# Attention rows split in their own layout and transposed by DMA, softmax taken earlier in VectorE's step, block maxima at five spread places

## The reference

```python
x = hidden                                   # (1, 2048, 1024)
# attention part: layernorm, q k v, and attention over the 32 HEADS of one token
n = layernorm(x)
q, k, v = (n @ w.T + b  reshaped to (S, 32, 32) for each of wq, wk, wv)
scores = einsum('bshd,bstd->bsht', q, k) / sqrt(32)
x = x + einsum('bsht,bstd->bshd', softmax(scores), v)
# feed-forward part: weights quantised to NF4 by blocks of 64 (absmax) and back
n = layernorm(x)
h = silu(n @ dq(w1).T) * (n @ dq(w2).T)      # 2752 wide
out = x + h @ dq(w3).T
```

## Time and profile before

| | us |
|---|---|
| median of 3 runs | 2148.68 |
| profiled execution, its own time | 2147.14 |
| span of the profiled execution | 2145.3 |
| busy: PE / DVE / ACT / POOL | 1989.0 / 1841.1 / 1492.3 / 1167.7 |
| first projection matmul | 87.29 |
| first feed-forward matmul | 721.15 |

### The profile page before, as it was taken

How to read it: one execution, slowest core, us unless ns; L and a number is a source line. 1 busy time by engine, 2 the same in 40 slices (tenths; PEclk the granted TensorE clock), 3 DMA queues, 4 the chain that set the end, 5 groups by cost and what they waited for, 6 DMA issues and landing times. The chain is left out here.

```text
span 2145.3 us, 30875 instructions
## 1 busy us (share of the span) xinstructions
PE 1989.0 (93%) x10272; PEld 1074.2 (50%) x10272; DVE 1841.1 (86%) x1846; ACT 1492.3 (70%) x1665; POOL 1167.7 (54%) x674
## 2 busy tenths in 40 slices
PE   5699999999987599999999999999999999999998
PEld 3477777776767244444444444444444444444442
DVE  8578888888878999898989989899998989989882
ACT  5424242424226697988989889797988979989782
POOL 0100101010111578788787787878787787787873
PEclk8799999999986699999999999999999999999999
DMA  7123433343322741212121212121212121212113
GB/s 284 58 77 113 142 113 128 116 137 113 122 74 98 267 126 40 59 39 52 45 53 45 59 39 59 39 59 39 59 39 59 39 53 45 59 40 55 35 35 157
DMA packets 219616, 175.24 MB, mean 82 GB/s; under 512 B 143664, under 2 KB 186672, under 8 KB 219568
## 3 DMA queue, kind: packets, MB, share of 16 engines
q1 hardware_dynamic: 217456, 166.23, 27.5%
q10 hardware_dynamic: 2112, 8.39, 1.0%
HBM read 115.34 MB, written 25.17 MB: 65 GB/s over the span
## 5 line engine op out<-in xcount | busy, mean ns | idle before, releaser
L1272 DVE SCALAR_TENSOR_TENSOR bank<-signs,bank 128x1024 f32<-128x1024 int8 (+2 forms) x792 | 964.4, 1218 | 102.2 <-ACT signs L1171 75.2
L1171 ACT ACTIVATE signs<-w_nat,compare_bias 128x1024 int8<-128x1024 f32 (+2 forms) x924 | 987.4, 1132 | 0.8 <-DVE w_nat L1272 0.6
L1402 PE MATMUL bank<-x2T_hi,w12T_hi 128*128 128x512 f16 x1376 | 524.2, 381 | 17.2 <-DVE hidden L1280 6.6
L1403 PE MATMUL bank<-x2T_lo,w12T_hi 128*128 128x512 f16 x1376 | 524.0, 381 | 0.0
L1404 PE MATMUL bank<-x2T_hi,w12T_lo 128*128 128x512 f16 x1376 | 523.8, 381 | 0.0
L772 PE MATMUL bank<-wT_hi,xT_hi 128*128 128x512 f16 x768 | 298.0, 388 | 12.2 <-issue 12.2
L772 PE MATMUL bank<-wT_hi,xT_lo 128*128 128x512 f16 x768 | 297.8, 388 | 0.0
L1423 PE MATMUL bank<-w3T_hi,hT_hi 128*128 128x512 f16 x704 | 272.3, 387 | 25.6 <-DVE hidden L1280 22.5
L727 ACT ACTIVATE probs<-probs 128x1024 f32<-128x1024 f32 x16 | 16.9, 1058 | 375.1 <-DVE probs L653 375.1
L1425 PE MATMUL bank<-w3T_hi,hT_lo 128*128 128x512 f16 x704 | 272.3, 387 | 0.0
L1424 PE MATMUL bank<-w3T_lo,hT_hi 128*128 128x512 f16 x704 | 271.7, 386 | 0.0
(11 more groups left out here) (96 smaller groups left out, 2670.9 us busy)
## 6 DMA issues: line engine op xcount, KB each, us to landing
ff_raw<-in_L_ffn_w SPq DMA_DIRECT2D x63, 512.0 KB, 3.7
w_nat<-in_L_ffn_w SPq DMA_DIRECT2D x63, 512.0 KB, 3.9
x_nat<-in_L_attn_hidden_states SPq DMA_DIRECT2D x16, 512.0 KB, 3.8
x_res<-in_L_attn_hidden_states SPq DMA_DIRECT2D x16, 512.0 KB, 4.4
x<-x_res SPq DMA_DIRECT2D x16, 512.0 KB, 2.6
acc<-x ACTq DMA_DIRECT2D x4, 2048.0 KB, 15.1
out<-acc SPq DMA_DIRECT2D x16, 512.0 KB, 2.6
w_raw<-in_L_attn_wq SPq DMA_DIRECT2D x8, 512.0 KB, 6.9
```

Of the source, the lines that this page charges most:

```text
L1171: nc.scalar.activation(signs[0:rows, ring(v, k), 0:cols], w_nat[0:rows, v % SLOTS, 0:cols], ACT.Sign, scale=COMPARE[SUMMED[k]][0], bias=co ...
L1272: V.scalar_tensor_tensor(to, part, HALF_STEP[SUMMED[k]], total, ALU.mult, ALU.add).then_inc(sign_used, 1)
L1402: nc.tensor.matmul(dst, hi, x2T_hi[:, toks, c], start=c == 0, stop=False)
L1403: nc.tensor.matmul(dst, hi, x2T_lo[:, toks, c], start=False, stop=False)
```

## The change

1. **Split as the rows lie, transposed by DMA.** The normalised tile is no longer transposed by TensorE. ScalarE writes its high half and GpSimd its low half, 128x1024 each, into x_half (`high_half`, `low_half`), and ScalarE starts two DMA transposes into xT_hi and xT_lo (`turn_x`). TensorE waits for them by `x_ready`. The layernorm's scale takes in X_SCALE (`moments`). For the finished tile the same two halves go to DRAM untransposed, and `load_tokens` transposes the four blocks of 512 tokens by DMA on their way back; x2T_hi and x2T_lo are laid out by block.
2. **VectorE's order.** Row maxima and subtraction come after the first evacuation of Q, ahead of `norm_apply`; the block transpose of the exponentials comes right after the second one; the second layernorm's apply comes after the transpose of Q. The two `split_lo` are gone. qkv has two slots instead of three: V takes that of Q, so the first evacuation of each waits for the other's block transpose.
3. **TensorE's order.** Context has banks 6 and 7, so that the scores wait for `ctx_read` no more. The 32 scores stand at 8 places of Q, after its 7th to 14th matmul, four at each. p_diag is written in two parts (eight instructions of 32x512) and the first 16 context products wait only for the first.
4. **Looks at named places**: early, centered, summed, key, value. Nine in steps 0 and 1 together, five and four in a loop turn, three in step T - 2.

The diff, cut to its core:

```diff
+        x_half = sb("x_half", [P, 2, E], F16)
...
+        def high_half(act, rows, half, done):
+            nc.scalar.activation(half[:, 0], rows, ACT.Copy).then_inc(done, 1)
+
+        def low_half(pool, rows, half, done):
+            nc.gpsimd.tensor_tensor(half[:, 1], rows, half[:, 0], ALU.subtract).then_inc(done, 1)
+
+        def turn_x(act, n, slot):
+            for i, (to, done) in enumerate(((xT_hi, x_hi_done), (xT_lo, x_lo_done))):
+                act.wait_ge(done, n + 1)
+                act.sem_inc(held, 1)
+                act.dma_start_transpose(to[:, slot], x_half[:, i]).then_inc(x_ready, 16)
...
-        mixing = bank[:, 4:6].rearrange("p b n -> p (b n)")
-        scores = mixing.rearrange("p (t h) -> p t h", h=HEADS)
-        context = mixing.rearrange("p (t d) -> p t d", d=HD)
+        scores = bank[:, 4:6].rearrange("p b n -> p (b n)").rearrange("p (t h) -> p t h", h=HEADS)
+        context = bank[:, 6:8].rearrange("p b n -> p (b n)").rearrange("p (t d) -> p t d", d=HD)
...
+        LOOK_PLACES = {5: "early centered summed key value", 4: "early centered summed value", 3: "early centered summed", 0: ""}
...
@@ sync, step @@
-                for look in todo[1:4]:
-                    load_ff(*look)
+                for place in ("centered", "summed", "key"):
+                    load_for(place)
                 if end and attend:
-                    sp.wait_ge(x2_turned, 2 * (n - 1))
+                    sp.wait_ge(x2_lo_done, n - 1)
                     load_res(sp, n - 1)
-                for look in todo[4:]:
-                    load_ff(*look)
                 if end:
-                    sp.wait_ge(x2_lo_done, 2 * n)
+                    sp.wait_ge(x2_lo_done, n - 1)
                     sp.sem_inc(held, 1)
-                    for dram, part in ((x2_hi_dram, x2_hi), (x2_lo_dram, x2_lo)):
...
+                        sp.dma_start(dram[bass.ds((n - 2) * P, P), :], x2_half[:, i]).then_inc(x2_out, 16)
+                load_for("value")
@@ gpsimd, step @@
+                if normalize:
+                    pool.wait_ge(x_hi_done, n + 2)
+                    low_half(pool, x_nat[:, 1 - u], x_half, x_lo_done)
...
                 if feed and attend:
                     next(feed)
+                if end:
+                    pool.wait_ge(x2_hi_done, n - 1)
+                    low_half(pool, x_res[:], x2_half, x2_lo_done)
@@ scalar, step @@
                 if normalize:
-                    split_hi(act, n + 1, xT_hi[:, 1 - u], x_turned, x_hi_done)
+                    act.wait_ge(normed, n + 2)
+                    act.wait_ge(x_ready, 32 * (n + 1))
+                    high_half(act, x_nat[:, 1 - u], x_half, x_hi_done)
...
-                    place(p_diag, flipped[:], p_placed)
+                    place(p_diag, flipped[:], p_placed, 2)
+                if normalize:
...
+                    turn_x(act, n + 1, 1 - u)
...
-                    split_hi(act, n - 2, x2_hi, x2_turned, x2_hi_done)
+                    act.wait_ge(normed2, n - 1)
+                    high_half(act, x_res[:], x2_half, x2_hi_done)
@@ tensor @@
+                    if early:
+                        skip, slots = 6, skip
...
-                        if end:
-                            pe.wait_ge(ctx_read, n - 1)
...
-                        pe.wait_ge(p_placed, n)
+                        pe.wait_ge(p_placed, 2 * n - 1)
                         pe.wait_ge(v_ready, n)
+                        if end:
+                            pe.wait_ge(ctx_read, n - 1)
                     for t in range(first, last):
+                        if t == QUAD // 2:
+                            pe.wait_ge(p_placed, 2 * n)
...
-                    turn(x_nat[:, 1 - u], x_turned)
...
-                    turn(x_res[:], x2_turned)
@@ feed_forward, sync @@
             def load_tokens(b):
-                tiles = slice(b * ST_BLOCK, (b + 1) * ST_BLOCK)
+                if b == 0:
+                    sp.wait_ge(g["x_ready"], 32 * T)
                 for part, dram in ((x2T_hi, x2_hi_dram), (x2T_lo, x2_lo_dram)):
-                    sp.dma_start(part[:, tiles].rearrange("p t c s -> p t (c s)"),
...
+                    sp.dma_start_transpose(part[:, b], dram[b * BANK:(b + 1) * BANK, :]).then_inc(x2_in[b], 16)
```

## The result

The changed kernel takes 2183.36 us (median of 4 runs, 2182.59 to 2185.4), the kernel before in the same session 2147.95 (2145.85 to 2148.92). The ratio is 1.0168 [1.015, 1.0185]: slower by 1.7%, where about 1% faster was forecast, and the time lies outside the range. Each profiled execution can be cut at the marks that the prediction used: VectorE's first reading of a context, the one of tile 14 (M), and the first sum of weight tile 3.

The account below looks back on a forecast made before the run. TensorE was taken to bound the attention steps before, the chain to VectorE's value look (33.5 us a step) after. 2147.14 - 44.0 (attention) + 20.8 (hand-over) = 2123.9 us profiled, so 2125 as median; range 2102 to 2158.

Parts of the forecast that it names:

- TensorE's step: Attention step: TensorE needs 32.2 us, 3.8 less than before, if nothing else is late.
- The chain to the value look: Attention loop: VectorE's last look waits for apply, halves, stores and load; period 33.5 us, TensorE waiting some 1.3.
- Rival E: Attention loop: TensorE's wait grows past what the clock bears, 8 to 10 us lost a step, over 2220 us; 4%.
- Steps 14 and 15: Last attention steps: idle stretch of 3.69 us and low clock go; 65.9 us instead of 81.0, 15.1 saved.
- The start: Before the first context: TensorE begins 2 us later, step 1 gives back its transpose; 0.7 us lost.
- The hand-over: From M to the first sum of weight tile 3: 109.7 us against 88.9, so 20.8 given back.
- two forms for this stretch: Hand-over: 87.3 + 4 tau; from tau about 7, last block and second weight transpose bind, near 76 + 6 tau.
- tau: Hand-over: time of each 1 MB token block's transposing load, taken as 5.6 us, ends 2.6 and twice 5.6.
- ScalarE's cover: Attention step: issuing two DMA transposes, 2.5 us, hides under p_diag's 4.7 us and costs nothing.
- rival D: Attention loop: the two transposes are not hidden on ScalarE; period 36.3 us, + 34, 2159 us in all; 13%.
- rival C: Hand-over: token blocks move at the rate of plain copies, 2.6 us each; 12 us less, 2113; 17%.

Follow-up runs that it names:

- e1: Kernel after, with SyncE issuing the value look's load ahead of the residual's load and the two stores: 2130.12 us, 0.9926 of before.
- e9: Kernel after, with the value look's load ahead of the two stores only, still behind the low-half wait and the residual's load: 2158.2 us.
- e6: On e1, VectorE makes the looks at the feed-forward scales behind the exponentials' transpose and the row sums in step T - 1: 2126.03 us.
- e3: Kernel after, with the first tile's low half made by VectorE instead of GpSimd: 2187.88 us, 1.0197 of before.
- e2: Kernel after, with token blocks read by plain copies instead of transposing ones (output differs, for timing only): 2179.72 us.
- e7: Kernel after with value load first, first low half on VectorE, x1 store ahead of token blocks 1 to 3, and scales later, together: 2125.47 us.
- e8: On e7, SyncE issues the four acc loads behind all token blocks, and a later weight tile's load ahead of blocks 2 and 3: 2110.96 us.
- e4: Kernel after, with TensorE doing the first 8 products of V's first half once more each attention step: 2165.52 us.

## Why the prediction was wrong

**TensorE's step: right.** 32.2 us were worked out (with 96 x 0.22 = 21.1, where the text has 20.7, it is 32.6), 32.37 measured, where nothing is late (e1).

**The chain to the value look: the right chain, sized 1.5 us short.** The prediction named it link by link from one context read to the next and came to 33.5. In the step shown above the apply ends at + 23.1 (22.6 forecast), the low half at + 26.6 (25.9), the value load is issued at + 28.5 (27.3), lands at + 33.9 (32.3) and the period is 35.0. No link is off by more than 0.5. But the wait on TensorE is what is left over, the period less TensorE's step: 33.5 - 32.2 = 1.3 was forecast and 34.96 - 32.37 = 2.6 came. 12 x (34.96 - 33.5) = 17.5 of the 41.2 us that the loop missed.

**The clock: the step that failed.** The prediction put falls of the clock in the loop at nothing. Rival E had them with 4%, "this needs two other misses", and with a fall in each step. The row with a wait of 1.84 and the mean clock of 0.98 made 1.3 look safe. What came was a fall in three of twelve steps, 7.9 us each: 23.7. e9 shows that the miss of the chain was not needed for it: its loop steps without a fall take 33.72 us, close to the forecast 33.5, which leaves 33.72 - 32.37 = 1.35 for TensorE's wait, and its profiled run has two falls all the same, at waits of 2.25 and 1.82 us. The prediction reasoned with the mean wait, and single waits are longer. The trace of before had a sign of this that the prediction did not use. Right behind the two longest of these waits in its loop, 2.13 us at 380.29 and 2.09 at 452.35, the clock is at 0.50 for some 3 us, and the 0.98 of the earlier trace rows is one of these two:

```profile
381.60:384.80 3.20, 3.20 (x9) 1.25 (x8) 3.20 (x4) 3.14 (x5) 0.00 (x0) 0.50 0.00 0
```

The chain's delay and the falls are cured by the same edit (e1), so the chain and not the new packing of scores, the halves of p_diag or the transposes on ScalarE is what made the loop slower.

**Steps 14 and 15: 9.9 us short** (75.8 against 65.9). Step T - 1 takes 44.23 us from context read to context read where 32.4, TensorE's step, was put; what is left for step 14 is 31.6, no more than the 33.5 forecast. The idle stretch ahead of the scores is gone as forecast. A new one of 2.91 us stands ahead of the context products, since VectorE's looks at the scales stand ahead of the exponentials' transpose, and the low clock of the earlier trace rows comes back some 20 us later, counted from M. This accounts for the smaller part: e6, without that wait, saves 3.9 us in this step (44.71 in e1, 40.80 in e6). The other 8.4 above a plain step are there in e6 too, where VectorE is what is late and makes the feed-forward pieces. That these pieces are the cause is read from that window; no run takes them out. The prediction saw such pieces and their order for step T, and for T - 1 it put them at nothing.

**The start: 4.4 short.** The low half was priced, what GpSimd does between it and the all-reduce was not (e3).

**The hand-over: 4.3 short, otherwise right.** The store of x1 goes out at M + 72.4 (72.9 forecast), the last apply starts at + 75.8 (75.5), ScalarE's high half at + 88.2 (88.0). A token block alone takes 4.4 us and not 5.6, but the first had 1.5 MB ahead of it and took 6.7. What was missed is behind that: ScalarE stands 7.61 us where it issues the loads of acc, before it was 2.93. The prediction's two forms for this stretch meet at a tau of 5.65 and not at about 7 (87.3 + 4 tau = 76 + 6 tau); at the 5.0 us that the four blocks take in the mean here the first holds, so nothing hung on that.

**ScalarE's cover (rival D): held.** The two transposes of a tile are issued beside p_diag, and the finished tile's high half starts when p_diag ends (396.89 in the step shown above):

```profile
395.29 1.47 ACTq L272 DMA_TRANSPOSE xT_lo<-x_half  x1
...
396.94 1.06 ACT L263 ACTIVATE x_half<-x_res 128x1024 f16<-128x1024 f32 x1
```

**The transposes' rate (rival C): nearer the forecast than plain copies.** The Trainium skill ("Advanced Engine Details and Errata", X-Bar Transpose (TRN2)) has transposes as fast as plain copies. Here a block of 1.05 MB out of DRAM takes 4.4 us, some 238 GB/s, and copying the blocks in e2 was worth 11 us; the rows bear out that they are slower than plain copies, less so than the 187 GB/s that the prediction took from SBUF.

What stays open: what decides whether a wait is followed by a fall (below).

## What to carry to other kernels

A load that an engine on the critical path will wait for goes into a queue ahead of everything that waits for a late producer: the queue takes over the latest wait in it. Where TensorE is left with a pause of some 2 us each step, count a fall of the clock as likely and not as a tail risk; here the falls cost 23.7 us in the loop, beside 30.6 of the late chain. A mean wait is not enough for that: look at the longest single ones, and at the clock right behind them, already in the trace of before. Large transfers with slack (acc here) are to be spread, since small urgent ones stand behind them: in e7 those of another queue, in e8 those of the same one.

## What the runs showed of the hardware

- The length of the wait alone does not say whether the clock falls. In the kernel after waits of 2.34, 2.71, 4.61 and 2.91 us were followed by 0.50, one of 2.31 was not, nor were 2.09 and 1.89. In e9 waits of 1.82 and 2.25 were, in e3 one of 2.32 was and one of 2.42 was not. In the kernel before, 2.13 and 2.09 were followed by some 3 us at 0.50 only, while the falls in the loops of after, e3, e4 and e9 last 17 to 24 us.
- GpSimd's all-reduce ran at once after 12.34 us of waiting (e3), and 5.94 us after the end of a subtraction (after). The root behind a memset came after 6.96 us (6.89 in the kernel before).
- A transpose's issue on SyncE takes as long as the queue's transfers let it: 4.1 to 5.0 us for 512x1024 as a rule, 6.70 with 1.5 MB ahead in its own queue, 25.07 with 8 MB of another queue's loads in the way.
- The stores of a tile's high half, 256 KB, landed after 4.0 us in the kernel after and 2.1 before, and the next tile's load after 6.2 instead of 3.9 (medians of two or three issues each, 300 to 400 us), with the same 126 GB/s in all.
